# Scores three units ahead of the context products, and other work at two seams, in a layer of FFN, attention and FFN on one core

## The chip, the core and the metric

The kernel runs on one core of a Trainium2 chip. The metric is the device time of one execution in microseconds (us). The engines are TensorE (PE, whose weight loads are PEld), VectorE (DVE), ScalarE (ACT), GpSimd (POOL) and the queues that issue transfers, above all SyncE's (SP). Each takes its own instructions in the order written and waits on semaphores for the others.

## What is computed

x has 2 x 1024 tokens of 1024 numbers. The layer is: x += 0.5 * FFN(norm(x)); x += Attn(norm(x)); x += 0.5 * FFN(norm(x)).

- FFN: a product with a 1024 x 1024 weight and a bias, and low-rank products of 8 experts, of which the two with the largest gate logits count.
- Attn: q = h Wq (32 heads of 32), k = h Wk and v = h Wv (8 heads), rotary embedding on q and k, causal softmax of q k / sqrt(32), its product with v, then Wo. Four q heads share one k and v head, so there are 2 x 8 = 16 groups; below a group is called a head, as in the kernel's loop over n (NG = 16).

## The kernel before, in words

`build` (L1787) runs four stages, each in a block of its own: `ffn_stage` "f1", `qkv_stage`, `attention_stage`, `ffn_stage` "f2". At the end of a block all engines meet (in the profile a wait of one engine's sequencer at the line of `nc.Block()` or of the function's `with`), and only then does the next one begin. The two meetings that the change touches are called seams: f1 to qkv, and qkv to attention. Products are made of high and low parts: `split_products` (L73 to L77) issues three matmuls for one product.

**f1.** Tiles of 128 tokens. SP stores each result tile from `x_ring` to x1 in HBM (L331). At the end SP waits until all stores have landed (L337), so the meeting does too. In f1's last four tiles `early` gets the first four tiles of x1, normalized, for the next stage.

**qkv.** Chunks of 512 tokens: `step(b, ch, ...)` goes through b = 0, 1 and ch = 0, 1, and through o = 0 to 9 (8 blocks of Wq's columns, 2 of Wk's), then four tiles of v. PE first turns (transposes) the four `early` tiles (L959), each of which ACT and DVE split into high and low (L1040, L1178); then it does the first two products by pairs of tiles (`by_pairs`), and then, before o = 2, it turns tile 4 (`turn_h`, L951). For that DVE must have normalized tile 4 (L1172), which takes ACT's square root (`deviation`, L1035). ACT has 8 instructions ahead of that one in its order: `for j in range(KC)`, L1073 to L1075, which split the rows of Wk and Wv into their high parts as they land in the two buffers `wkv_raw`; POOL makes the low parts (L1122 to L1125), and SP loads rows j after the low part of j - 2 is done (L925). Wk is first needed at o = 8. At its end ACT loads the table of the exponential (L1113) and waits until v is stored (L1116).

**attention.** One head is 10 units, `units` (L1326): parts of the scores of four q heads (g = 0 to 3) with up to 512 queries and 128 or 256 keys. For a unit PE makes four scores (`scores`, L1587), ACT four exponentials (`exps`, L1678), POOL masks the units on the diagonal (0, 1, 2, 7, 8, 9; L1498), and PE makes the context products (`products`, L1604) and, after units 2 and 9, the row sums (`sums`, L1623 and L1627). The scores of a unit are made `AHEAD` units before its products:

```python
    PROBS = 6
    AHEAD = 2
        HELD = (1, 3, 5, 7)
```

Six units' exponentials have a place in `probs`. At step u, PE issues scores of unit u + AHEAD and, between them, rows of scores of the next heads (`slot_item`, L1576), whose maxima DVE takes (`row_maximum`, L69) from four PSUM banks, `SLOTS` = 4; the scores use `BANKS` = 3 others. Then it issues the products of unit u. Those of a unit in `HELD` wait for the next step and go with that unit's:

```python
                    if u - 1 in HELD:
                        products(n, u - 1)
                    if u not in HELD:
                        products(n, u)
```

POOL's order in a head is: mask of unit u + AHEAD at each step where there is one, `join` at u = 1 (L1526), `divide` at 2 and 8 (L1504), the additions of the exponentials of units 3 to 7 at u = 2, 3, 5, 6, 7 (`add`, L1519), `low_wo` at 9 (L1530). The sums after unit 9 need these additions. In the last head DVE makes them (L1765), and there are no more rows. The row maxima of a head come back, turned and negated, as two rows of its q (`load_rows`, L1442, two for each half of the queries). The scores of unit 0 wait for those of the first half, those of unit 3 for those of the second (L1584). The turn for the second half (`TURN_B`) is made at step 9 of the head before.

Of the kernel before, what the change touches and what calls it, by code (L numbers as in the profile page):

```python
# [99 lines left out]
def ffn_stage(nc, name, x_src, x_dst, base_b, consts, ident, chunk_loaded, prep=None, attn=None):  # L100
# [7 lines left out]
    with ExitStack() as ctx:  # L108
# [5 lines left out]

        fw = ffn_weights(nc, ctx, name)
# [13 lines left out]
        x_ring = sb("x_ring", [P, 4, D], F32)  # L129
# [148 lines left out]
        def _(sp):  # L278
# [33 lines left out]
            def step(i, t, u, more):  # L312
# [18 lines left out]
                sp.dma_start(x_dst[bass.ds(t * P, P), :], x_ring[:, u, :]).then_inc(stored[u], 16)  # L331
# [4 lines left out]
            for s in range(4):  # L336
                sp.wait_ge(stored[s], 16 * (NT // 4) + (16 if s == 3 else 0))  # L337
# [40 lines left out]
        def _(pe):  # L378
# [131 lines left out]
            run_tiles(pe, step)  # L510

# [267 lines left out]
def qkv_stage(nc, x_src, wq, early, heads, w, consts, ident, scr):  # L779
# [10 lines left out]
    with ExitStack() as ctx:  # L790
# [25 lines left out]
        v_out = sb("v_out", [P, 2, KV], F32)  # L816
# [43 lines left out]
        v_stored = [sem(f"v_stored{s}") for s in range(2)]  # L860
# [22 lines left out]
        def run_chunks(eng, step):  # L883

            with eng.Fori(0, B - 1, 1) as b:
                for ch in range(NCH):
                    step(b, ch, True)
            for ch in range(NCH):
                step(B - 1, ch, ch + 1 < NCH)

        @block.sync
        def _(sp):
# [23 lines left out]

            sp.dma_start(cos[:], consts["rope_cos"]).then_inc(const_loaded, 16)
            sp.dma_start(sin[:], consts["rope_sin"]).then_inc(const_loaded, 16)
            for j in range(KC):
                if j == WRAW:  # L920
                    sp.wait_ge(h_turned, TC + 1)
                    for slot in range(2):
                        load_x(TC + slot, slot)
                if j >= WRAW:
                    sp.wait_ge(wkv_lo_done, j - WRAW + 1)  # L925
                for cols, src in ((slice(0, KV), w["Wk"]), (slice(KV, 2 * KV), w["Wv"])):
                    sp.dma_start(wkv_raw[:, j % WRAW, cols], src[j * P:(j + 1) * P, :]).then_inc(wkv_loaded[j % WRAW], 16)
            with sp.Fori(TC // 2 + 1, NT // 2, 1) as i:
                for slot in range(2):
                    load_x(2 * i + slot, slot)  # L930
# [16 lines left out]
        def _(pe):  # L947
# [79 lines left out]
            for b in range(B):  # L1027
                for ch in range(NCH):
                    step(b, ch, b + 1 < B or ch + 1 < NCH, done=0 if b or ch else 2)

        @block.scalar
        def _(act):
# [40 lines left out]
            for j in range(KC):  # L1073
# [10 lines left out]
            def step(b, ch, more):  # L1084

                act.wait_ge(v_done, b * (NCH * TC) + (ch * TC + 1))
                for o in range(NO):
                    g = ch * NO + o
                    if not more and o and TURN_A in items_of(o):
# [9 lines left out]

                for s in range(TC):  # L1100
# [12 lines left out]
            act.activation(std[:], eps[:], ACT.Exp)  # L1113
            for s in range(2):
                act.wait_ge(out_stored[s], B * NCH * NO * 16 + 16)
                act.wait_ge(v_stored[s], B * NCH * TC * 8 + 16)  # L1116

        @block.gpsimd
        def _(pool):
            pool.memset(eps[:], EPS).then_inc(eps_set, 1)  # L1120
            pool.sem_inc(lo_done, 2)
            for j in range(KC):  # L1122
# [10 lines left out]
            def chunk_step(b, g):  # L1133
# [731 lines left out]
```

## Time and profile before

| what | us |
|---|---|
| runs shown: median of 3 (lowest to highest) | 1537.8 (1535.55 to 1539.06) |
| the profiled execution's own time | 1538.84 |
| its span in the trace | 1537.1 |
| PE busy in it | 1496.4 |
| POOL, DVE, ACT busy in it | 697.9, 952.0, 581.1 |

The span is from the first to the last instruction of the program. The rows of the trace give each instruction its start and its busy time in us; a matmul's end is modelled and lies behind the start of the next, so that where PE waits is read from the starts of its instructions, and a PE shown as busy may still wait a little between them. "xN" behind a row is the number of instructions merged in it. A bracket at a row's end is the engine's idle time before it and what released it. A table by windows shows stretches of the span with each engine's busy time and the clock that was granted to PE (1.00 is 2.4 GHz, 0.50 is 1.2 GHz).

### The profile page before, as it was taken

The numbers are of one execution on the slowest core, as the hardware profiler recorded it, in microseconds if no ns is written. First come the engines' busy times: TensorE is split into PE (matmuls) and PEld (weight loads), VectorE is DVE, ScalarE is ACT, GpSimd is POOL, SyncE is SP. The second block draws the span as 40 slices with busy tenths as digits, with TensorE's granted clock in tenths as the row PEclk, the third lists the DMA queues.
The fourth block names the chain that finished last, engine by engine and source line by source line (L and its number), as shares of the span: only waits on it lengthen the run. The fifth ranks groups of instructions, "written<-read, shape, count | busy, mean of one in ns | idle before, by whom it ended". The sixth has DMA issues, their size and how long they took to land. (4 is left out here: it accounts for less than half of the span.)

```text
span 1537.1 us, 25937 instructions
## 1 busy us (share of the span) xinstructions
PE 1496.4 (97%) x9184; PEld 1190.8 (77%) x9184; DVE 952.0 (62%) x2726; ACT 581.1 (38%) x1058; POOL 697.9 (45%) x384
## 2 busy tenths in 40 slices
PE   7899998899999989999999999999999999999999
PEld 7899998788888875555555555555489999999988
DVE  6545454564654767888888888888555434343433
ACT  4233332221211026666666666666632212121210
POOL 1232322442434337899989989999603001010100
PEclk9999999899999998999999999999999999999999
DMA  6323233433424352444333344430161212121201
GB/s 236 127 99 113 98 125 114 135 112 108 143 77 131 97 143 66 99 103 99 84 78 77 77 97 103 101 84 23 54 243 42 82 42 83 42 82 41 82 14 42
DMA packets 118725, 146.01 MB, mean 95 GB/s; under 512 B 40896, under 2 KB 77120, under 8 KB 118336
## 3 DMA queue, kind: packets, MB, share of 16 engines
q1 hardware_dynamic: 90304, 121.37, 27.6%
q10 hardware_dynamic: 28304, 23.14, 4.6%
q8 instruction: 66, 1.08, 0.3%
q14 instruction: 51, 0.42, 0.1%
HBM read 95.72 MB, written 53.51 MB: 97 GB/s over the span
## 5 line engine op out<-in xcount | busy, mean ns | idle before, releaser
L1678 ACT ACTIVATE at_probs<-ps 128x512 f32<-128x512 f32 (+1 forms) x640 | 315.0, 560 | 172.4 <-PE ps L1587 165.5
L69 DVE CUSTOM_DVE_ANT_0 ps<-ps,at_score_mask 128x512 f32<-128x512 f32 (+2 forms) x480 | 269.9, 621 | 25.9 <-PE ps L1576 22.2
L348 POOL TENSOR_TENSOR f_x_ring<-f_x_ring,f_half_bias 128x1024 f32<-128x1024 f32 x32 | 78.2, 2445 | 309.3 <-DVE f_h L634 303.1
L1519 POOL TENSOR_TENSOR at_added<-at_added,at_probs 128x2048 f32<-128x2048 f32 (+1 forms) x60 | 210.3, 3506 | 2.7 <-ACT at_probs L1678 0.7
L1604 PE MATMUL ps<-at_probs,at_vs 128*32 128x512 f32 (+3 forms) x1536 | 144.6, 494 | 0.3 <-POOL at_probs L1498 0.3
L75 PE MATMUL f_ps<-f_wt_hi,f_hT_hi 128*128 128x400 f32 (+1 forms) x384 | 134.1, 349 | 3.2 <-DVE f_hT_lo L638 3.2
L76 PE MATMUL f_ps<-f_wt_lo,f_hT_hi 128*128 128x400 f32 (+1 forms) x384 | 131.6, 343 | 0.0
L75 PE MATMUL ps<-f_wt_hi,f_hT_hi 128*128 128x400 f32 (+1 forms) x384 | 131.5, 343 | 0.0
L77 PE MATMUL f_ps<-f_wt_hi,f_hT_lo 128*128 128x400 f32 (+1 forms) x384 | 131.5, 342 | 0.0
L76 PE MATMUL ps<-f_wt_lo,f_hT_hi 128*128 128x400 f32 (+1 forms) x384 | 130.3, 339 | 0.0
L77 PE MATMUL ps<-f_wt_hi,f_hT_lo 128*128 128x400 f32 (+1 forms) x384 | 130.1, 339 | 0.0
L69 DVE CUSTOM_DVE_ANT_0 ps<-ps,at_score_mask,at_part_max 128x128 f32<-128x128 f32 (+3 forms) x240 | 120.9, 552 | 13.7 <-issue 13.5
L673 DVE TENSOR_TENSOR f_x_ring<-ps,f_x_ring 128x512 f32<-128x512 f32 x32 | 21.8, 690 | 137.7 <-PE ps L77 125.1
L1498 POOL TENSOR_SCALAR_AFFINE_SELECT at_probs<-at_probs 128x512 f32<-128x512 f32 (+1 forms) x96 | 80.8, 842 | 57.4 <-ACT at_probs L1678 57.4
L75 PE MATMUL ps<-wide_hi,shared 128*128 128x512 f32 x256 | 101.2, 395 | 1.6 <-DVEq L703 1.1
L1136 POOL TENSOR_TENSOR qkv_rot<-qkv_rot,qkv_sin 128x512 f32<-128x512 f32 x40 | 51.5, 1290 | 112.1 <-DVE qkv_rot L1222 112.1
L1587 PE MATMUL ps<-heads 98*128 98x512 f32 (+3 forms) x288 | 95.9, 377 | 5.4 <-PEq L1559 3.9
L77 PE MATMUL ps<-wide_hi,shared 128*128 128x512 f32 x256 | 99.9, 390 | 0.0
L76 PE MATMUL ps<-wide_lo,shared 128*128 128x512 f32 x256 | 99.8, 390 | 0.0
L352 POOL TENSOR_TENSOR wide_lo<-f_wq_raw,wide_hi 128x512 f32 (+1 forms) x16 | 23.6, 1474 | 161.4 <-ACT wide_hi L531 161.4
L1047 ACT ACTIVATE qkv_rope_hi<-qkv_rope 128x512 fp32r<-128x512 f32 x40 | 25.3, 632 | 185.2 <-DVE qkv_rope L1183 172.5
L1604 PEld LDWEIGHTS ps<-at_probs,at_vs 128*32 128x32 f32 x1536 | 40.3, 109 | 61.5 <-issue 44.7
(202 smaller groups left out, 3623.8 us busy)
## 6 DMA issues: line engine op xcount, KB each, us to landing
f_x_ring<-in_L_attn_resid SPq DMA_DIRECT2D x16, 512.0 KB, 3.6
x<-f_x_ring SPq DMA_DIRECT2D x16, 512.0 KB, 2.7
early<-x SPq DMA_DIRECT2D x16, 512.0 KB, 3.3
scr_q_hi<-qkv_rope_hi ACTq DMA_DIRECT2D x32, 256.0 KB, 2.0
scr_q_lo<-qkv_rope_lo ACTq DMA_DIRECT2D x32, 256.0 KB, 2.3
scr_ctx<-at_ctxn SPq DMA_DIRECT2D x32, 256.0 KB, 2.4
shared<-scr_ctx SPq DMA_DIRECT2D x16, 512.0 KB, 4.5
f_x_ring<-x SPq DMA_DIRECT2D x16, 512.0 KB, 3.7
```

The lines of the kernel that those rows point to most:

```text
L69: return dve.tensor_tensor_reduce(out=src[:, 0:keys], in0=src[:, 0:keys], in1=mask, scale=1.0, scalar=part_max[:, g, own] if c else -3.0e3 ...
L75: pe.matmul(out, stat_hi, mov_hi, start=start, stop=False)
L76: pe.matmul(out, stat_hi, mov_lo, start=False, stop=False)
L77: return pe.matmul(out, stat_lo, mov_hi, start=False, stop=stop)
L348: pool.tensor_tensor(x_ring[:, u, :], x_ring[:, u, :], half_bias[:], ALU.add).then_inc(bias_added, 1)
L1047: act.activation(rope_hi[:, g % 2, :], rope[:, g % 2, :], ACT.Copy).then_inc(hi_done, 1)
L1136: pool.tensor_tensor(rot[:, g % 2, :], rot[:, g % 2, :], sin[:, cols], ALU.mult).then_inc(sin_done, 1)
L1498: pool.affine_select(out=tile, in_=tile, compare_op=ALU.is_ge, fill=0.0, base=0, pattern=[[0, G], [0, count], [1, P]], channel_multiplier= ...
L1519: pool.tensor_tensor(added[:, heads, :], first, probs[:, (NU * n + u) % PROBS, heads, :], ALU.add).then_inc(added_done, 1)
L1587: last = pe.matmul(score_ps[x % BANKS][:, cols], ks[:, nm, j * P:(j + 1) * P], q_stack(n)[0:KROWS + 2, half, g, at], start=True, stop=True)
L1604: last = pe.matmul(ctx_ps[g * DH:(g + 1) * DH, at], vs[:, n % RING, j, :], probs[:, (NU * n + u) % PROBS, g, cols], start=j == 0, stop=u i ...
L1678: act.activation(probs[:, (NU * n + u) % PROBS, g, cols], score_ps[x % BANKS][:, cols], ACT.Exp, scale=SCALE).then_inc(exp_done, 1)
```

## The change

- attention: `AHEAD` is 3, `HELD` is (1, 3).
- f1 to qkv: the store of f1's last tile counts on a semaphore of its own, `x_stored`. f1 no longer waits for it; SP waits for it at the start of qkv, before its loads of constants, weights and x. PE makes 16 transposes of the identity at the end of f1. `x_ring` is placed first in f1's memory.
- in qkv: the high and low parts of Wk and Wv are made within the steps of the first chunk, j = 0 and 1 at o = 0, j = o + 1 at o = 1 to 6. SP loads tiles 6 and 7 of x ahead of rows 4 and 6 of the weights. Loops over b are written out.
- qkv to attention: SP waits for the stores of v at the start of attention, after two loads, and no more at the end of qkv; `v_out` is placed so that it outlives the stage. ACT loads the exponential's table before the last four tiles of v. PE makes 16 transposes at the end of qkv.

The diff, cut to its core:

```diff
@@ ffn_stage
+        x_ring = sb("x_ring", [P, 4, D], F32)
         fw = ffn_weights(nc, ctx, name)
...
-        x_ring = sb("x_ring", [P, 4, D], F32)
...
-                sp.dma_start(x_dst[bass.ds(t * P, P), :], x_ring[:, u, :]).then_inc(stored[u], 16)
+                own = x_stored if prep and isinstance(t, int) and t == NT - 1 else stored[u]
+                sp.dma_start(x_dst[bass.ds(t * P, P), :], x_ring[:, u, :]).then_inc(own, 16)
...
-                sp.wait_ge(stored[s], 16 * (NT // 4) + (16 if s == 3 else 0))
+                sp.wait_ge(stored[s], 16 * (NT // 4) + (16 if s == 3 and not prep else 0))
...
             run_tiles(pe, step)
+            if prep:
+                for _ in range(WARM):
+                    pe.transpose(hT_ps[:, 0, :], ident[:], ident[:])
@@ qkv_stage
-            with eng.Fori(0, B - 1, 1) as b:
+            for b in range(B):
                 for ch in range(NCH):
-                    step(b, ch, True)
-            for ch in range(NCH):
-                step(B - 1, ch, ch + 1 < NCH)
+                    step(b, ch, b + 1 < B or ch + 1 < NCH)
+        def weights_of(b, g):
+            if b or g >= KC - 1:
+                return ()
+            return (0, 1) if g == 0 else (g + 1,)
...
+            sp.wait_ge(x_stored, 16)
             sp.dma_start(cos[:], consts["rope_cos"]).then_inc(const_loaded, 16)
...
+                if j in (WRAW + 2, WRAW + 4):
+                    load_x(TC + j // 2, j // 2 % 2)
...
+            pe.wait_ge(cos_done, B * NCH * NO + 4)
+            for _ in range(16):
+                pe.transpose(ps[:, 2, 0:P], ident[:], ident[:])
...
-            for j in range(KC):
+            def high_weight(j):
                 act.wait_ge(wkv_loaded[j % WRAW], 32 * (j // WRAW + 1))
                 act.activation(wkv_hi[:, j, :], wkv_raw[:, j % WRAW, :], ACT.Copy).then_inc(wkv_hi_done, 1)
...
                     g = ch * NO + o
+                    for j in weights_of(b, g):
+                        high_weight(j)
...
+                if not more:
+                    act.activation(std[:], eps[:], ACT.Exp)
...
-            act.activation(std[:], eps[:], ACT.Exp)
             for s in range(2):
                 act.wait_ge(out_stored[s], B * NCH * NO * 16 + 16)
-                act.wait_ge(v_stored[s], B * NCH * TC * 8 + 16)
...
             def chunk_step(b, g):
+                    for j in weights_of(b, g):
+                        low_weight(j)
@@ attention_stage
-    AHEAD = 2
+    AHEAD = 3
...
-        HELD = (1, 3, 5, 7)
+        HELD = (1, 3)
...
                 load_v(r)
+            for stored in v_stored:
+                sp.wait_ge(stored, NT * 8 + 16)
```

## Rows read from the trace of the kernel before

**Rows 1.** The page's first part: busy time, share of the span, instructions.

```profile
PE 1496.4 (97%) x9184; PEld 1190.8 (77%) x9184; DVE 952.0 (62%) x2726; ACT 581.1 (38%) x1058; POOL 697.9 (45%) x384
```

**Rows 2.** Windows: stretch, length, busy PE, PEld, DVE, ACT, POOL, clock, DMA share, GB/s.

```profile
262.20:266.35 4.15, 0.00 (x0) 0.03 (x1) 0.57 (x2) 0.00 (x0) 0.10 (x1) 0.80 0.31 126
266.35:272.50 6.15, 6.15 (x33) 6.10 (x34) 2.45 (x2) 2.83 (x3) 0.00 (x0) 0.58 0.73 256
284.15:291.60 7.45, 0.00 (x0) 0.03 (x1) 1.78 (x4) 2.07 (x4) 4.54 (x4) 0.80 0.24 72
291.60:295.40 3.80, 3.80 (x13) 3.40 (x14) 3.70 (x6) 0.07 (x1) 2.52 (x2) 0.50 0.42 138
```

**Rows 3.** Timelines at the first seam; the row of 446.00 is eight transposes at full clock.

```profile
261.92 0.27 PE L77 MATMUL f_ps<-f_bt_hi,f_lowT_lo 128*128 128x224 f32 x1
...
262.80 0.35 SPq L331 DMA_DIRECT2D x<-f_x_ring  x1
...
269.45 1.22 DVE L1178 TENSOR_TENSOR heads<-qkv_ps,heads 128x1024 fp32r<-128x1024 f32 x1 [6.68 <-ACT heads L1040]
...
272.37 0.39 PE L75 MATMUL qkv_ps<-heads,wide_hi 128*128 128x256 f32 x1
...
446.00 1.04 PE L959 MATMUL qkv_ps<-ident,early 128*128 128x128 f32 x8
```

**Rows 4.** ACT and PE in qkv, up to the turning of tile 4.

```profile
268.39 1.02 ACT L1040 ACTIVATE heads<-qkv_ps 128x1024 fp32r<-128x1024 f32 x1 [8.91 <-PE qkv_ps L959]
...
289.47 0.28 ACT L1035 ACTIVATE qkv_std<-qkv_mv,qkv_eps 128x1 f32<-128x1 f32 x1
...
291.60 1.94 PE L959 MATMUL qkv_ps<-ident,early 128*128 128x128 f32 x8 [7.46 <-issue]
```

**Rows 5.** The second seam: windows, then ACT's and PE's timeline.

```profile
570.73:574.61 3.88, 0.00 (x0) 0.03 (x1) 0.00 (x0) 1.87 (x3) 0.59 (x2) 1.00 0.33 52
574.61:581.51 6.90, 6.76 (x23) 5.17 (x23) 1.80 (x11) 5.29 (x12) 1.35 (x2) 0.55 0.87 195
581.51:585.60 4.09, 4.09 (x15) 2.23 (x15) 1.76 (x8) 1.30 (x3) 3.06 (x2) 0.51 1.08 259
...
571.17 0.38 ACTq L1064 DMA_DIRECT2D scr_v<-qkv_v_out  x1
...
581.51 1.94 PE L1604 MATMUL ps<-at_probs,at_vs 128*32 128x512 f32 x8
```

**Rows 6.** One steady head as a window, from the end of one head's sums to the next.

```profile
886.12:919.69 33.57, 33.27 (x255) 19.23 (x251) 29.28 (x104) 21.61 (x45) 30.55 (x16) 1.00 0.40 88
```

**Rows 7.** PE and DVE in that head: products of two units, DVE's two longest pauses.

```profile
906.68 1.92 PE L1604 MATMUL ps<-at_probs,at_vs 128*32 128x512 f32 x16
...
909.38 0.63 DVE L69 CUSTOM_DVE_ANT_0 ps<-ps,at_score_mask,at_part_max 128x384 f32<-128x384 f32 x1 [0.87 <-issue]
...
919.92 0.72 DVE L1735 STREAM_TRANSPOSE at_sumT<-ps 128x512 f32<-128x512 f32 x1 [2.11 <-issue]
```

**Rows 8.** POOL's longest pause between two additions in that head.

```profile
904.94 0.68 POOL L1498 TENSOR_SCALAR_AFFINE_SELECT at_probs<-at_probs 128x512 f32<-128x512 f32 x1 [0.76 <-ACT at_probs L1678]
```

**Rows 9.** The rows that come back: issue, transfer time, and PE's next scores.

```profile
DMA to landing us min/median/max: 1.8/1.8/2.5
...
917.61 0.59 SPq L1442 DMA_DIRECT2D shared<-at_neg_lo  x1
...
919.69 0.44 PE L1587 MATMUL ps<-shared,heads 98*128 98x256 f32 x2
```

**Rows 10.** The last head on PE.

```profile
1101.88 0.96 PE L1587 MATMUL ps<-heads 98*128 98x512 f32 x3
...
1107.20 0.91 PE L1587 MATMUL ps<-heads 98*128 98x256 f32 x6
...
1108.68 1.71 PE L1604 MATMUL ps<-at_probs,at_vs 128*32 128x512 f32 x16
...
1111.39 1.04 PE L1623 MATMUL ps<-at_added,at_ones 128*32 128x512 f32 x8
```

More of the change, by code:

```diff
@@ L97, in flat, with ffn_stage @@
     return tile[:, :, :].rearrange("p c n -> p (c n)") if len(tile.shape) == 3 else tile[:, :]
-def ffn_stage(nc, name, x_src, x_dst, base_b, consts, ident, chunk_loaded, prep=None, attn=None):
+def ffn_stage(nc, name, x_src, x_dst, base_b, consts, ident, chunk_loaded, prep=None, attn=None, x_stored=None):
     RAW = 3
@@ L776, in _, with qkv_stage @@
             run_tiles(dve, step)
-def qkv_stage(nc, x_src, wq, early, heads, w, consts, ident, scr):
+def qkv_stage(nc, x_src, wq, early, heads, v_out, w, consts, ident, scr, x_stored, v_stored):
     NCH = T // HALF
@@ L815, in qkv_stage @@
         rope_lo = sb("rope_lo", [P, 2, HALF], F32R)
-        v_out = sb("v_out", [P, 2, KV], F32)
         q_stacks = [hT_hi[0], flat(wq_lo)[:, KC * HALF:].rearrange("p (b n) -> p b n", n=HALF)]
@@ L859, in qkv_stage @@
         v_copied = sem("v_copied")
-        v_stored = [sem(f"v_stored{s}") for s in range(2)]
         first_head_loaded = sem("first_head_loaded")
@@ L927, in _ @@
                     sp.dma_start(wkv_raw[:, j % WRAW, cols], src[j * P:(j + 1) * P, :]).then_inc(wkv_loaded[j % WRAW], 16)
-            with sp.Fori(TC // 2 + 1, NT // 2, 1) as i:
-                for slot in range(2):
-                    load_x(2 * i + slot, slot)
+            for t in range(TC + 4, NT):
+                load_x(t, t % 2)
             sp.wait_ge(v_done, (B * NCH - 1) * TC + 1)
@@ L1121, in _, with low_weight @@
             pool.sem_inc(lo_done, 2)
-            for j in range(KC):
+            def low_weight(j):
                 pool.wait_ge(wkv_hi_done, j + 1)
@@ L1140, in chunk_step @@
                         low_part(b, g)
-            with pool.Fori(0, B - 1, 1) as b:
+            for b in range(B - 1):
                 for g in range(NCH * NO):
@@ L1235, in _, with attention_stage @@
             run_chunks(dve, step)
-def attention_stage(nc, consts, ident, scr, wo, wo_src, heads, shared, ps):
+def attention_stage(nc, consts, ident, scr, wo, wo_src, heads, shared, ps, v_stored):
     RING = 3
@@ L1803, in build @@
     over = ExitStack()
+    x_stored = whole.enter_context(nc.semaphore("x_stored"))
+    v_stored = [whole.enter_context(nc.semaphore(f"v_stored{s}")) for s in range(2)]
     with ExitStack() as ctx:
         early = ctx.enter_context(nc.sbuf_tensor("early", [P, 4, D], F32))
-        ffn_stage(nc, "f1", x, x1, base_b, consts, ident, chunk_loaded, prep={"wq": wide, "early": early, "Wq": ins["L0_attn_Wq"], "copy": copy, **raw})
+        ffn_stage(nc, "f1", x, x1, base_b, consts, ident, chunk_loaded, prep={"wq": wide, "early": early, "Wq": ins["L0_attn_Wq"], "copy": copy, **raw},
+                  x_stored=x_stored)
         heads = over.enter_context(nc.sbuf_tensor("heads", [P, 2, KC, HALF], F32R, side="right"))
-        qkv_stage(nc, x1, wide, early, heads, attn_w, consts, ident, scr)
+        v_out = over.enter_context(nc.sbuf_tensor("v_out", [P, 2, NKV * DH], F32, side="right"))
+        qkv_stage(nc, x1, wide, early, heads, v_out, attn_w, consts, ident, scr, x_stored, v_stored)
     with ExitStack() as ctx:
@@ L1811, in build @@
         ps = ctx.enter_context(nc.psum_tensor("ps", [P, 8, HALF], F32))
-        attention_stage(nc, consts, ident, scr, wide, ins["wo_rows"], heads, shared, ps)
+        attention_stage(nc, consts, ident, scr, wide, ins["wo_rows"], heads, shared, ps, v_stored)
         over.close()
```

## Prediction, written before the changed kernel was run

> **What bounds the kernel now.** I read the page first: PE is busy for 97% of the span and no other engine for more than 62% [rows 1]. So time is won only where PE stands still, runs at the lower clock, or is spread out by waits between its instructions. I then read the windows around the seams and the timelines inside them, and last one head of attention.
>
> PE stands still in three places. Between f1 and qkv it has nothing for 4.15 us, and then works for 6.15 us at a mean clock of 0.58 [rows 2]. Its last matmul starts at 261.92; the last store of x is issued at 262.80 [rows 3]. Inside qkv it stands for 7.45 us and then runs 3.80 us at clock 0.50 [rows 2]. Between qkv and attention it stands for 3.88 us and then works until 585.60 at 0.55 and 0.51 [rows 5].
>
> In attention one head takes 33.57 us. PE shows 33.27 us busy, POOL 30.55, DVE 29.28, ACT 21.61 [rows 6]. PE's figure hides waits, as its ends are modelled. DVE's rows are what it waits for: within the head DVE pauses for only 33.57 - 29.28 = 4.29 us. The two largest pauses are 2.11 us before the sums of unit 9, and 0.87 us right after PE has gone through the products of two units, 16 instructions in 1.92 us, in which no row is made and DVE uses up its four banks [rows 7].
>
> **First seam, 3.2 us.** The meeting now waits for the landing of the last store, issued at 262.80. After the change the last to arrive is PE itself: its 16 transposes cost, by the eight in 1.04 us at full clock, about 0.11 us each when pipelined, so 1.8 us, to about 263.9 [rows 3]. The store's issue ends at 263.15 and lies beside it. A meeting takes 0.6 to 0.9 us; nearest to it is the gap from the store's landing to 266.35. I take 0.75: PE begins qkv at 264.6, not at 266.35, 1.75 us earlier. Then the first pair of products waits for two tiles to be split: eight transposes (1.04), one copy by ACT (1.02) [rows 4], two subtractions by DVE (1.22 each) [rows 3], 4.5 us in all with the hops: 269.15, where it was 272.37 [rows 3]. That is 3.2 us. If the clock still falls, only the 1.75 us remain. SP waits for the landing before it loads constants; that is no later than it was, so it costs nothing. The 16 transposes have the store's landing as their cover before the change and none after it: they are the price of the clock, 1.8 us, already in the sum. Did the meeting wait for anything else that I don't see, the lower end is 0.
>
> **The pause inside qkv, 9.35 us.** ACT comes to the square root for tile 4 only at 289.47, after its eight parts of Wk and Wv; tile 4 is turned at 291.60 [rows 4]. Moved into the steps, six of the eight stand behind that root. Tile 4 of x can be normalized long before 284. So all 7.45 us go, and with them the 3.80 us at half clock, which cost half of it, 1.90 [rows 2]. What is late next: Wk at o = 8, six blocks of Wq's columns later. Every copy is made a step ahead of POOL's subtraction and SP's next load, and ACT, POOL and SP have pauses in each step; SP is now held by the waits for tiles 6 and 7, with only weights behind them. Cover gone, one weight late would cost about a step. I take 9.35, bounds 7.45 and 9.35. The written-out loops I cost at nothing: branches stand beside PE's work.
>
> **Second seam, 2.5 us.** ACT issues the last store of v at 571.17 [rows 5], and the meeting waits for its landing. Now PE's 16 transposes, to 572.5, come last, and attention begins at about 573.5, not 574.61, 1.1 us earlier. With three units ahead there are 16 exponentials, not 12, before the first products. ACT spends 5.29 us on 12, 0.44 each [rows 5]; PE is let go three banks before the end, after 13: 0.5 + 13 x 0.44 = 6.2 us, so products at 579.7, where they were at 581.51: 1.8 us. The head then ran at half clock until 585.60, 4.09 us [rows 5], of which 2 us come back if the clock holds. If it falls, the rows between the scores take some 0.5 more as well. That is 1.3 to 3.8; since PE is only half busy in that prologue I take 2.5, midway.
>
> **The steady heads, 13.05 us.** Units 5 and 7 no longer wait for the next one, so PE gives 8 product instructions at a time where it gave 16, about 1 us in place of 1.92. Four waiting rows of about 0.63 us cover that, and the pause of 0.87 us goes [rows 7]. DVE sets the pace in this stretch, so I take it whole; the 2.11 us before the sums stay, as the order around unit 9 is unchanged. The added cost is two more changes between kinds of work on PE, 0.1 to 0.2 us each, hidden by DVE; without that cover 0.35 us a head. POOL gets its masks' inputs a unit earlier and loses its pause of 0.76 us [rows 8], so its 30.55 us don't bind at 32.7. Fifteen heads have rows beside them: 15 x 0.87 = 13.05 us. The bounds for a head are a loss of 0.35 and a gain of 1.5 (DVE's pauses other than the 2.11 cut to some 0.7).
>
> **The last head, 1.9 us.** No rows there: ACT paces the scores. From 1101.88 to 1111.39 are 9.51 us [rows 10]. After: four scores (1.3), products of 5 (0.95), four scores (1.5), products of 6 (0.95), then those of 7 to 9, 1108.68 to 1111.39, 2.71: 7.4. Four wider scores at its step 0 give 0.2 back. Between 0 and 2.5.
>
> **Sum.** 3.2 + 9.35 + 2.5 + 13.05 + 1.9 = 30.0 us. The profiled execution took 1538.84, 1.0 above the median of the runs: 1508.8. f2 is PE at full clock and moves along with it.
>
> **A rule against the change.** In the stretch 266.35 to 272.50 PE had nothing but transposes until 272.37, and its mean clock was 0.58, so it rose from 0.50 to 1.00 before the stretch ended [rows 2, 3]. The Trainium skill, "TensorE: Matmul & The Clock Gate", Part 4, says that the full clock doesn't engage for transposes, which don't count as PE busy. By the trace they do count; by the rule the 16 would be time spent for nothing, and the seams would stay cold, as in the second rival.
>
> **The rivals.**
> - *Nothing in the steady heads.* The pause of 0.87 us goes and comes back elsewhere, before the sums, since PE, DVE and POOL all lie within 10% of each other [rows 6]. Then 1538.84 - 16.95 = 1521.9.
> - *The clock falls at both seams all the same.* For it: PE is half busy in attention's prologue. Against it: pauses of under 1 us, where those of 3.88 us and more had it fall. The first seam gives 1.75, the second 1.3: 1538.84 - 27.35 = 1511.5.
> - *More in the heads.* DVE never pauses but for 2.11 + 0.6 us: 32.0 us a head, 1.5 saved each: 1538.84 - 16.95 - 22.5 = 1499.4.
> - *Slower: the rows that come back.* The scores of unit 3 are now made at step 0, right behind the sums. They wait for two small transfers: issued at 917.61, 1.8 us on the way, so 919.4, against PE's first scores at 919.69 [rows 9]. The margin is 0.3 us. If DVE comes to that turn four rows (2.6 us) later against PE, every head waits 2.3 us: 1538.84 - 16.95 + 15 x (2.3 - 0.87) = 1543.3. From 2.0 us a head on it decides. Against it: the turn itself waits for DVE, so PE can't run far ahead.
> - *The change doesn't do what it says.* A meeting may wait for another landing, and a mask made sooner may hold POOL's additions; gains and losses then cancel.
>
> **How the numbers follow.** Chances: forecast 0.55; nothing in the heads 0.17; clock falls 0.13; more in the heads 0.10; slower 0.03; cancelling 0.02. The range reaches from 1499 to 1523, over the first three and most of the fourth. What a measurement tells from no change is about 0.2%, 3 us. Faster by more: 0.95; within: 0.02; slower: 0.03.
>
> **What would show it.** PE's last f1 matmul and first qkv transpose under 3 us apart, at clock 1.00; no pause of 7 us before tile 4; the first products of attention 14.4 us earlier than at 581.51 (3.2 + 9.35 + 1.8), near 567; heads of 32.7 us with DVE's pause of 0.87 gone and that of 2.11 kept; POOL without the 0.76. Wrong it would be if heads stay at 33.6, if PE pauses before unit 3's scores (L1587) behind the sums, or if unit 9's sums wait for POOL.

## The result, and the profile after

The changed kernel takes 1519.2 us by the median of 4 runs (1518.3 to 1520.0), the kernel before on the same chip 1536.7: a ratio of 0.9887, 95% interval 0.9872 to 0.9902. The gain is 17.5 us, where 30.0 were forecast (1508.8); the range of 1499 to 1523 holds it. The profiled execution took 1518.7 us, its span is 1517.0. The gain between the two profiled executions is 20.1, and 3.0 of that lie in f1, ahead of everything that the prediction counted: PE waits once for DVE before the small transpose of `low_s`, for 3.14 us in the trace before and for 1.64 in the one after, and behind the longer wait the clock is at 0.5 for 3.4 us. f1's instructions up to there are the same, only the place of `x_ring` in memory isn't. Of the twelve traces with the changed kernel's f1 two have that fall (e5 and e6), of the two with the f1 of before both (e2 is the other). So the change may have a part in it; two traces are too few to tell. The 3.0 us are kept apart below.

By the page's first part PE is busy for 1487.0 us, where it was 1496.4 [rows 1]. It has 32 instructions more (the transposes) and yet is busy 9.4 us less: matmuls at the lower clock count as busy for longer, and there are fewer of them.

The windows of the changed kernel that answer to [rows 2] and [rows 5], and one head, which answers to [rows 6] (columns as there; the break leaves out qkv, the last line is the head):

```profile
259.16:261.51 2.35, 1.75 (x18) 1.54 (x15) 0.58 (x2) 0.00 (x0) 0.10 (x1) 1.00 0.38 157
261.51:266.14 4.63, 3.69 (x32) 3.44 (x32) 2.41 (x3) 3.46 (x4) 0.00 (x0) 1.00 0.63 222
...
557.84:558.73 0.89, 0.00 (x0) 0.03 (x1) 0.00 (x0) 0.00 (x0) 0.59 (x2) 1.00 0.58 87
558.73:567.46 8.73, 8.45 (x28) 6.20 (x28) 1.81 (x11) 7.34 (x16) 2.45 (x3) 0.63 0.95 199
867.89:900.98 33.09, 32.77 (x255) 19.53 (x251) 29.37 (x104) 21.26 (x45) 30.55 (x16) 1.00 0.41 89
```

The first seam is warm now. The second is not: attention begins after only 0.89 us, and still its prologue has a mean clock of 0.63. A head is 0.48 us shorter, not 0.87. PE's timeline at the end of f1 and inside qkv:

```profile
259.00 1.91 PE L514 MATMUL f_ps<-ident 128*128 128x128 f32 x16
...
266.14 0.39 PE L75 MATMUL qkv_ps<-heads,wide_hi 128*128 128x256 f32 x1 [0.95 <-DVE heads L1196]
...
277.76 0.49 PE L967 MATMUL qkv_ps<-ident,early 128*128 128x128 f32 x3
...
491.24 0.33 PE L1001 MATMUL qkv_ps<-heads 96*128 96x128 f32 x1 [0.82 <-DMA qkv_wkv_raw<-in_score_mask]
```

How it is read, with the 3.03 us of f1 taken off each time (f1's last product starts 3.03 us earlier, 258.89 against 261.92):

- qkv begins at 261.51, 1.81 us sooner; its first pair of products at 266.14, where it was 272.37: 3.20 sooner.
- Tile 4 is turned at 277.76, without a pause, where it was 291.60: another 7.6. The stretch behind it, which ran at half clock before, gives 1.8 more (the same matmul stands at 295.46 before and at 279.81 after). Together 9.4.
- The row at 491.24 is a wait that the kernel before hardly had: PE stands before the first row of the next stage's first head. The transfers that bring that head are issued as much earlier as PE is (the mask at 481.22, where it was 496.82), but the one that lands last, the mask, takes 9.97 us where it took 9.01. It costs 1.0 us of what had been won: the distance to the kernel before falls from 15.65 us ahead of it to 14.64 behind it.
- Attention begins 15.9 us earlier than at 574.61 as the clock shows it, 12.8 without f1's part: 3.2 + 9.4 - 1.0 + 1.2.
- The first products of attention come 8.73 us after its start. Before it was 6.90, and I had forecast 6.2.

DVE in the steady head, answering to [rows 7]:

```profile
887.67 0.70 DVE L69 CUSTOM_DVE_ANT_0 ps<-ps,at_score_mask 128x512 f32<-128x512 f32 x1 [0.29 <-PE ps L1596]
...
901.22 0.72 DVE L1755 STREAM_TRANSPOSE at_sumT<-ps 128x512 f32<-128x512 f32 x1 [2.02 <-issue]
```

The pause of 0.87 us is down to 0.29 and not gone, that before the sums (2.11 us before) is still there, and POOL's pause before a mask [rows 8] is gone: POOL's longest is now 1.70 us before the join of unit 1, waiting for PE's products. In this head DVE's pauses fell from 4.29 us to 3.72 and its busy time rose by 0.09; the head lost 0.48. What can't be seen in these rows is what sets a head's length now, and which of the two edits of attention did it. The runs answer the second and part of the first.

In what follows a head's length is taken from the end of one head's last sums to the end of the next head's (the last one runs to the first product behind attention). By this measure the 14 steady heads took 470.7 us before and 464.7 after (33.62 and 33.20 each), the first one 42.04 and 43.59, the last one 26.88 and 27.10.

### The profile page after: what moved, and what is told of

It reads as the page before. It is cut to its first block and busy times, and to the rows that moved or that the text cites. A ratio compares the mean times of both kernels' runs of the same rounds, so it can differ in the third digit from the quotient of the medians.

```text
span 1517.0 us, 25951 instructions
## 1 busy us (share of the span) xinstructions
PE 1487.0 (98%) x9216; PEld 1192.2 (79%) x9216; DVE 954.8 (63%) x2726; ACT 576.2 (38%) x1058; POOL 700.9 (46%) x384
## 5 line engine op out<-in xcount | busy, mean ns | idle before, releaser
L1698 ACT ACTIVATE at_probs<-ps 128x512 f32<-128x512 f32 (+1 forms) x640 | 311.1, 560 | 169.4 <-PE ps L1607 164.1
L1624 PE MATMUL ps<-at_probs,at_vs 128*32 128x512 f32 (+3 forms) x1536 | 152.1, 500 | 0.7 <-POOL at_probs L1518 0.7
L1607 PEld LDWEIGHTS ps<-heads 98*128 98x128 f32 x288 | 52.9, 197 | 44.4 <-ACT at_probs L1698 25.1
```

Source lines behind the costliest of these rows:

```text
L1607: last = pe.matmul(score_ps[x % BANKS][:, cols], ks[:, nm, j * P:(j + 1) * P], q_stack(n)[0:KROWS + 2, half, g, at], start=True, stop=True)
L1624: last = pe.matmul(ctx_ps[g * DH:(g + 1) * DH, at], vs[:, n % RING, j, :], probs[:, (NU * n + u) % PROBS, g, cols], start=j == 0, stop=u i ...
L1698: act.activation(probs[:, (NU * n + u) % PROBS, g, cols], score_ps[x % BANKS][:, cols], ACT.Exp, scale=SCALE).then_inc(exp_done, 1)
```

## The experiments

### Which part gave what: e1 and e2

e1 is the changed kernel with attention as it was; e2 is the kernel before with attention's edits alone.

```diff
 e1, on the changed kernel            e2, on the kernel before
-    AHEAD = 3                        -    AHEAD = 2
+    AHEAD = 2                        +    AHEAD = 3
-        HELD = (1, 3)                -        HELD = (1, 3, 5, 7)
+        HELD = (1, 3, 5, 7)          +        HELD = (1, 3)
```

> The changed kernel with attention as before (two units ahead, four held). My theory: the parts add up. Read from the two traces, attention begins 3.2 + 9.4 - 1.0 + 1.2 = 12.8 us earlier through the seams' edits (the 1.0 is the new wait in qkv's last chunk), and with two units ahead its first head costs what it did before, so the gain over the kernel before is 12.5 to 13.5 us: about 1523.7 us. Rival A: the loss in the first head (1.55 us) comes from the seam, not from the third unit ahead; then the gain is 11.3. Rival B: the seams' edits give less by themselves, because attention's own edits shift the first store of v or the meeting: under 10. Heads of 33.6 us in every case.

> The kernel before with attention's two edits alone (three units ahead, two held). My theory: 14 heads that each give 0.42 us, a last head and a first head that lose what they lose in the changed kernel: a gain of 4 to 6 us, about 1532 us, heads of 33.15 us. As forecast blind it would have been 13.05 + 1.9 + 1.8 = 16.8 us. Rival: the heads are faster by 0.87 us when they start at another phase of the transfers, a gain over 10 us. Rival: the first head loses nothing here since the cold start of the old seam is paid anyway; then the gain is 6 to 7.

e1: 1526.9 us against 1537.8, ratio 0.9926 (0.9904 to 0.9949), a gain of 10.9. e2: 1530.9 us, ratio 0.9944 (0.9924 to 0.9963), a gain of 6.9. Together 17.8, against the change's 17.5: the parts add up, within their intervals. e1's gain is under what I expected, and its trace shows where: its first head takes 41.73 us, as before, so rival A is wrong, but its last takes 30.24 us instead of 26.88, with the clock at 0.5 twice, from 1076.7 and from 1090.3, each time for 3.4 us. e2 gained a little more than the 4 to 6 us that I expected: its steady heads take 463.7 us for 14, 0.50 less each, the first head 1.1 us more than before and the last 1.0 us less. So the seams give some 11 to 13 us, attention's edits the other 5 to 7.

### Which edit of attention: e3 and e4

Both are the changed kernel with one of the two taken back.

```diff
 e3                                   e4
-        HELD = (1, 3)                -    AHEAD = 3
+        HELD = (1, 3, 5, 7)          +    AHEAD = 2
```

> The changed kernel with units 5 and 7 held again (1, 3, 5, 7), scores still three units ahead. Theory of the prediction: the pause of 0.87 us of DVE comes from the held pair, so it comes back and heads are at 33.5 to 33.6 us: 5 to 7 us slower than the changed kernel. Rival: the third unit ahead alone gives the gain, since PE's scores stand ready and ACT's late exponentials no longer stop it; then it is within 2 us of the changed kernel, and so is the pair's pause in heads of 33.1 us.

> The changed kernel with scores two units ahead, units 5 and 7 still not held. Theory of the prediction: the pair's products are split in two, DVE's pause of 0.87 us goes, but products of units 5 and 7 come a step earlier behind their own exponentials, which lie only two units back, so PE waits for ACT or for POOL's masks in steps 5 and 7; that wait is worth what the pause was: heads between 33.1 and 33.6 us. In the first head it gains 1.5 us against the changed kernel (12 exponentials before the first products, not 16). Rival: the third unit isn't needed at all, heads of 33.1 or under, and the kernel is 1 to 3 us faster than the changed one.

e3: 1525.7 us, ratio 0.9926 (0.9903 to 0.9950). e4: 1518.1 us, ratio 0.9875 (0.9844 to 0.9905). A head's window in e3 and in e4, and under it the row of DVE that answers to the one with 0.87 in [rows 7], first for e3:

```profile
839.32:873.01 33.69, 33.40 (x251) 19.70 (x250) 29.32 (x104) 21.55 (x45) 30.44 (x16) 1.00 0.38 87
...
862.59 0.63 DVE L69 CUSTOM_DVE_ANT_0 ps<-ps,at_score_mask,at_part_max 128x384 f32<-128x384 f32 x1 [0.87 <-issue]
```

and then for e4:

```profile
864.91:897.98 33.07, 32.79 (x254) 19.37 (x250) 29.42 (x104) 21.41 (x45) 30.64 (x16) 1.00 0.38 89
...
884.72 0.70 DVE L69 CUSTOM_DVE_ANT_0 ps<-ps,at_score_mask 128x512 f32<-128x512 f32 x1 [0.33 <-PE ps L1596]
```

With four units held, the pause of 0.87 us is back to the hundredth, and the third unit ahead gives the steady heads nothing: 33.81 us each over 14, against 33.65 in e1. With two held and scores only two units ahead it is down to 0.33, and the heads take 33.15 us, as in the changed kernel. **The whole gain in the heads is that of the two holds given up.** The third unit costs in the first head: it took 43.5 us with it (e3, and 43.59 in the changed kernel) and 41.1 to 41.7 without it (e4, e1), about 2 us. In the last head it gives back 1.2 where the clock holds (25.5 in e3, 26.7 in e4). For e4 the rival was right about the heads, and my expectation that units 5 and 7 would then wait for ACT was wrong. That e4 as a whole is the faster kernel isn't shown: its four runs lie at 1514.3, 1514.9, 1521.3 and 1522.4 us, and its interval covers the changed kernel's.

### Who paces a steady head: e5 to e8

Each is the changed kernel with one engine's work in 12 or 14 heads made longer or shorter. e6 leaves out the spreading of the reciprocals in heads 2 to 13, so their context isn't divided by their own sums.

```diff
 e5, DVE, behind the rows of step 6; e8 the same on POOL
+                    if 0 < n < NG - 1 and u == 6:
+                        dve.memset(spare[:], 0.0)
 e6, DVE, in reciprocal
-                dve.transpose(recip[:], recipT[:].broadcast_to([P, HALF // DH, DH])).then_inc(recip_done, 1)
+                if 1 < n < NG - 2:
+                    dve.sem_inc(recip_done, 1)
+                else:
+                    dve.transpose(recip[:], recipT[:].broadcast_to([P, HALF // DH, DH])).then_inc(recip_done, 1)
 e7, PE, in products, ahead of those of unit 0
+                if u == 0 and 0 < n < NG - 1:
+                    for g in range(G):
+                        pe.matmul(ctx_ps[g * DH:(g + 1) * DH, :], vs[:, n % RING, 0, :], probs[:, NU * n % PROBS, g, :],
+                                  start=True, stop=True)
```

> The changed kernel with one more operation of DVE in 14 heads, a memset of a spare tile of 128x512 behind the rows of step 6; nothing waits for it. In the changed kernel a head takes 33.06 to 33.1 us in its shortest form, with DVE 29.37 and PE 32.77 us busy. Theory A (DVE still paces the rows, as the prediction had it): the head grows by the whole of that operation, 0.3 to 0.6 us as its row will show. Theory B (with the pair's pause gone PE is the bound, its products, scores and rows running at the pace of their own columns): the operation is hidden in DVE's remaining 3.7 us of pauses and the head grows by under 0.1 us.

> The changed kernel in which heads 2 to 13 leave out the transpose that spreads the reciprocals of the sums (two in each head, 0.7 us each), so that the context of these heads isn't divided by its own sums; POOL's multiplication and all waits stay. Theory A (DVE paces the head): up to 1.4 us less a head, 31.7. Theory B (PE is the bound): under 0.2 us less, and DVE's pauses grow by the 1.4.

> The changed kernel in which PE makes the four products of unit 0 twice in 14 heads (the same result, 0.43 us more at full clock if four instructions take what the four of a 512-wide group do in the trace). Theory A (DVE paces): hidden but for what lies behind DVE's own waits: the head grows by under 0.15 us. Theory B (PE is the bound): it grows by 0.35 to 0.45 us.

> The changed kernel with one more operation of POOL in 14 heads, a memset of a spare tile of 128x512 at step 6 (0.53 us by the like row of the prologue). POOL is busy for 30.55 of 33.09 us and stands 1.7 us before the join, where it waits for PE. Both theories: hidden, under 0.1 us a head. Rival C (POOL's additions set when the sums come, so that POOL shares the pace): 0.3 to 0.5 us a head.

One run each; the times (1522.3, 1517.8, 1534.8 and 1520.5 us) aren't compared, since f1's fall stands in two of them (e5 and e6), so only the heads are read. A window of one of the shorter heads in each, in the order e5, e6, e7 and e8:

```profile
838.34:871.64 33.30, 32.83 (x254) 19.46 (x251) 29.59 (x105) 21.24 (x45) 30.53 (x16) 1.00 0.38 89
```

```profile
868.96:901.93 32.97, 32.65 (x255) 19.47 (x251) 28.18 (x102) 21.25 (x45) 30.61 (x17) 1.00 0.39 90
```

```profile
880.65:914.55 33.90, 33.57 (x263) 19.75 (x259) 29.39 (x104) 21.22 (x45) 30.59 (x16) 1.00 0.38 87
```

```profile
835.14:868.42 33.28, 32.90 (x255) 19.66 (x251) 29.37 (x104) 21.21 (x45) 31.02 (x17) 1.00 0.39 89
```

Against 33.09: e5 makes a head 0.21 us longer, e6 0.12 shorter, e8 0.19 longer, e7 0.81 longer here. On the mean of all 14 steady heads (33.20 in the changed kernel) e5 and e8 cost 0.14 each, e6 gives 0.11, e7 costs 1.25 (about 0.8 in the first and in the last six, 1.2 to 2.2 in the seven between). Read with the busy time of DVE: in e5 it grew by 0.22 us, less than the memset's 0.485, whose ends overlap the rows beside it, and the head by about as much. In e6 it fell by 1.19 and the head by a tenth of that; DVE's pauses grew from 3.7 to 4.8 us. So of more work on DVE most of what adds to its busy time is paid, and less of it gives almost nothing: something else holds a head at 33.0 us. Of POOL's 0.52 us 0.19 is paid, against my expectation.

That PE's own work is the floor isn't shown. PE's busy figure counts modelled ends. From start to start a 512-wide score or row takes 0.23 us in that head and four 512-wide products side by side 0.45; by such steps all of PE's instructions come to some 29 us of the 33.09 (an estimate from the trace's starts). The rest are 0.1 to 0.2 us at each change between kinds of work, and waits: the weight loads of the scores wait for ACT's exponentials for 3.1 us in that window. No run changed ACT's work, so ACT's exponentials, which free the scores' three banks, stay an untested rival for the pace.

Where the rest of e7's loss comes from is seen in part on DVE. The first row is from the changed kernel, at the row behind the products of unit 0; the second is its like in e7:

```profile
871.67 0.57 DVE L69 CUSTOM_DVE_ANT_0 ps<-ps,at_score_mask 128x384 f32<-128x384 f32 x1 [0.52 <-PE ps L1596]
```

```profile
885.26 0.57 DVE L69 CUSTOM_DVE_ANT_0 ps<-ps,at_score_mask 128x384 f32<-128x384 f32 x1 [1.36 <-PE ps L1596]
```

While PE gives products, DVE uses up its four banks and then stands, and what it then lacks, PE waits for later. My reading is that a longer group of products is paid once on PE and again in part when DVE has to catch up, and that the holds work in the same way: 16 products in 1.92 us left DVE without rows for 0.87 us, twice 8 in 1.0 us leave it for 0.29. Neither theory holds as a whole: DVE's added work costs less than theory A says and more than theory B, DVE's removed work gives what theory B says, and PE's added work costs twice what theory B says.

The seven heads of e7 that lose 1.2 us and more have another wait. Each of them begins with one of 0.5 to 1.2 us at its first score, for the negated rows that come back:

```profile
707.25 0.50 PE L1607 MATMUL ps<-shared,heads 98*128 98x512 f32 x1 [0.74 <-DMA shared<-at_neg_lo]
```

This is the wait of the prediction's slower rival. In the changed kernel PE stands there in one head alone, for 0.40 us.

### No hold at all: e11

```diff
-        HELD = (1, 3)
+        HELD = ()
```

> The changed kernel in which no unit's products are held back to the next step (units 1 and 3 too). By the four kernels already run, giving up two of the four holds is worth 0.49 us a head, and the third unit ahead is worth nothing; the reason that I draw from the traces is that PE then gives its products in shorter groups and DVE isn't left without rows. If so, the pauses of DVE of 0.5 us (behind the products of units 0 and 1) shrink too: heads of 32.8 to 33.0 us. Rival: unit 1 is held because its mask and the join of POOL lie there; PE then waits for POOL and a head is 0.5 us or more longer. Since PE's own work is near its floor (32.97 us a head with 1.4 us of DVE's work taken away), nothing under 32.7 is expected.

One run: 1536.7 us, as slow as the kernel before. A head:

```profile
844.70:879.22 34.52, 33.46 (x251) 19.30 (x251) 29.42 (x104) 21.48 (x45) 30.47 (x16) 1.00 0.36 85
```

The rival's time is right, and more than right: 1.4 us more a head. Its reason is so in part: the weight loads of PE's products wait twice for POOL's masks in that window, 0.7 us in all, and not at all in the changed kernel's. POOL stands before the join for 2.9 us (1.7 in the changed kernel), but there it is POOL that waits for PE, and PE's scores stand behind ACT's exponentials for 4.6 us (3.1). The loss is 0.3 us up to the first half's sums, 0.3 in steps 3 and 4, 0.8 in step 5, and none behind it. In step 5 PE waits for DVE, in nearly every head and not in the changed kernel:

```profile
863.61 0.50 PE L1596 MATMUL ps<-heads 96*128 96x512 f32 x1 [0.71 <-DVE at_row_max L69]
```

Behind the products of unit 3, now given by themselves, DVE had stood for 1.25 us (at 859.06). So there a group given early leaves DVE without rows, and "shorter groups are better" holds for units 5 and 7 alone. Whether the hold of unit 1 or that of unit 3 matters more was not run.

### The transposes at the seams: e9

e9 is the changed kernel without the 16 transposes behind f1 and the 16 behind qkv.

```diff
-            if prep:
-                for _ in range(WARM):
-                    pe.transpose(hT_ps[:, 0, :], ident[:], ident[:])
...
-            for _ in range(16):
-                pe.transpose(ps[:, 2, 0:P], ident[:], ident[:])
```

> The changed kernel without the 16 transposes behind f1 and the 16 behind qkv. In the changed kernel's profile the first 16 run from 259.00 to 260.91, qkv begins at 261.51 and its first products at 266.14, and the clock stays at 1.00 until attention's prologue. Theory A (the transposes hold the clock): qkv begins 0.5 to 0.9 us earlier, since now the issue of the last store of x (about 260.1) comes last, but the clock falls behind f1 and the first products come 1.5 to 3 us later than with them. Theory B (the short pause is enough, the transposes are 1.8 us spent for nothing, which is also what comes out if transposes don't count as work for the clock): no fall at the first seam, first products 0.5 to 0.9 us earlier. At the second seam the clock falls in the prologue with them as without: attention begins about 1 us earlier by both.

One run, 1514.7 us. Behind f1:

```profile
259.92:261.84 1.92, 0.00 (x1) 0.03 (x1) 0.59 (x2) 0.00 (x0) 0.10 (x1) 1.00 0.25 100
261.84:266.48 4.64, 3.69 (x33) 3.46 (x33) 2.42 (x3) 3.47 (x4) 0.00 (x0) 1.00 0.66 234
```

PE stands for 1.92 us and the clock doesn't fall. From f1's last product's end to the first pair it is 6.56 us, where the changed kernel takes 6.98 (259.16 to 266.14): theory B, 0.4 us gained by leaving them out. The same edit in e12 below did have a fall of 3.4 us there, and took 7.03. So the first set is worth next to nothing: 6.98 us with it, against 6.56 without it when the clock holds and 7.03 when it falls. At the second seam the clock falls without them 0.4 us into attention, with them 2.3 us into it; the first products come 8.73 us after the start in both, and attention begins 0.6 us sooner after qkv's last product (1.98 us, not 2.6).

### Holding the clock in attention's prologue: e10

e10 has two units ahead (as e4), two transposes behind each of the prologue's eight scores, and the mask's load moved ahead of the first head's queries.

```diff
-    AHEAD = 3
+    AHEAD = 2
...
                     scores(0, u, g)
+                    for _ in range(2):
+                        pe.transpose(slot_ps[0][:, 0:P], ident[:], ident[:])
...
+            sp.dma_start(score_mask[:, HALF:MASK], consts["score_mask"]).then_inc(first_head_loaded, 16)
             load_queries(0, first_head_loaded)
             load_keys(0, first_head_loaded)
-            sp.dma_start(score_mask[:, HALF:MASK], consts["score_mask"]).then_inc(first_head_loaded, 16)
```

> The changed kernel with scores two units ahead, with two transposes of PE behind each of the first eight scores of attention's prologue (into a slot that the rows use later), and with the load of the mask ahead of the first head's queries instead of behind its keys. Theory A (the clock falls in the prologue since PE is only half busy between ACT's exponentials): a score and two transposes are 0.43 us against ACT's 0.48, so the clock holds, the first head takes 2.5 to 3.5 us less than the 41.14 us of the like kernel without them, and the wait before the first row in qkv's last chunk goes from 0.8 to 0: 1514.5 us or less by the median, 3.5 to 4.5 us under the kernel with two units ahead alone (1518.07). Theory B (the fall comes from the pause before attention, 0.9 us, and not from the half-busy prologue, or transposes don't count): the clock falls at the same place, the transposes then cost up to 0.2 us each, and the first head is 1 to 2 us longer.

1512.8 us by the median, ratio 0.9844 (0.9827 to 0.9860). That is 5.3 us under e4's median, but e4's runs lie 8 us apart; what the transposes do is read from the traces. The prologue in e4, and behind it in e10 a window nearly as long (both from attention's start; in e10 it takes in the first products too):

```profile
558.46:565.36 6.90, 6.67 (x23) 4.97 (x23) 1.81 (x11) 5.30 (x12) 1.35 (x2) 0.64 0.92 198
```

```profile
559.94:566.44 6.50, 6.50 (x47) 5.16 (x47) 2.22 (x14) 5.29 (x12) 1.66 (x3) 1.00 0.93 189
559.94:598.93 38.99, 38.14 (x280) 23.32 (x280) 29.70 (x113) 25.58 (x53) 30.36 (x16) 1.00 0.33 71
```

Theory A is right: the granted clock stays at 1.00 from 15.8 us to the end of the span, and the first head takes 38.99 us where it took 41.14, a little less of a gain than the 2.5 to 3.5 us expected. In attention nothing was added but small transposes between the scores, and e12 below, with the mask's load in its old place, holds the clock there too, so here they do keep it up. The rule of the Trainium skill that the prediction weighed ("TensorE: Matmul & The Clock Gate", Part 4) says they would not; by it the prologue of e10 should have been as cold as e4's, and the measurement decides. The mask's move did nothing: the wait before the first row is 1.0 us, since now the keys land last, at 492.40, 10.0 us after their issue; in the changed kernel the mask had come 10.0 us after its own. That time isn't fixed: the last of the seven took 8.9 us in e9 and 7.9 in e12, and there PE has no such wait. What sets it stays open.

### The best of it: e12

e12 is e10 with the mask's load back in its place, without the transposes behind f1, and with the rows of qkv's last chunk begun one product later.

```diff
-            if prep:
-                for _ in range(WARM):
-                    pe.transpose(hT_ps[:, 0, :], ident[:], ident[:])
...
-                            if 1 <= c <= len(own):
-                                row_item(own[c - 1])
+                            late = 2 if o == ROW_FROM else 1
+                            if late <= c < len(own) + late:
+                                row_item(own[c - late])
```

> The changed kernel with two units ahead and with two transposes behind each of the first eight scores of attention's prologue, as in the run that held the clock through the whole of the second seam (1512.78 by the median); the mask's load is back in its place, the 16 transposes behind f1 are gone (those behind qkv stay), and the rows in qkv's last chunk start one product later in their first block. Theory: from the look without transposes, qkv begins 0.4 us sooner behind f1 and the clock holds; the wait of 0.8 to 1.0 us before the first row is covered by the 0.75 us of one product: together 1.0 to 1.3 us, so 1511.5 to 1512 us by the median and at least 24 us under the kernel before. Rival A: the clock falls behind f1 in part of the executions, since nothing keeps PE at work there; then 1513 to 1515 us, and a wider spread. Rival B: the wait before the first row moves with the rows, since DVE is behind; then the gain is 0.4 us.

1511.5 us by the median of 5, ratio 0.9842 (0.9825 to 0.9859) against the kernel before. That beats both kernels: the changed one had 0.9887 (0.9872 to 0.9902), and the intervals don't meet. From e10 it can't be told apart. In its profile the wait before the first row is gone, but the later rows aren't shown to be the reason: the mask landed at 489.29, and the first row, at 490.75, would have come at about 490.06 without the product put ahead of it. And the clock fell behind f1, after PE had stood from 258.94 to 260.86:

```profile
260.86:265.97 5.11, 5.11 (x32) 5.11 (x33) 2.45 (x2) 2.94 (x3) 0.00 (x0) 0.67 0.71 252
```

The same pause of 1.92 us as in e9, and another outcome; the fall costs 0.5 us here (5.11 against 4.64), since the stretch behind it mostly waits for DVE and ACT. Rival A is right in its mechanism; its price was small. Two of e12's five runs took 3 us more than the others (1514.5 and 1514.7 against 1511.1 to 1511.5); they have no trace. A fall in f1, worth 3.0 us, would fit them, and so this isn't rival A's range coming true.

## Why the prediction was right, and where it failed

The range held the result; the likeliest value was 10.4 us too low. Luck had a part in the range. The forecast started from an execution that had f1's fall, and the changed kernel's profiled one did not: with it, it would stand near 1522, at the range's upper end. In the same way the sign "first products near 567" was met (567.46) with 3.0 us of f1's in it; without them the products came 11.0 us earlier, not 14.4. The terms against what the traces show, f1's 3.0 us left out:

| term | forecast | measured |
| --- | --- | --- |
| first seam, to the first pair | 3.2 | 3.2 |
| pause inside qkv | 9.35 | 9.4 |
| wait for the first head's loads | none | -1.0 |
| second seam: attention begins | 1.1 | 1.2 |
| second seam: to the end of the first head | 1.4 | -1.55 |
| steady heads | 13.05 | 5.9 |
| last head | 1.9 | -0.2 |
| sum | 30.0 | 17.0 |

(The measured terms and f1's 3.0 give 20.0, the two profiles 20.1. The forecast of 13.05 was for 15 heads, the first one among them; the measured 5.9 are 14 heads, and the first head stands in the row above.)

- **First seam: right, by its own steps.** The start came 1.81 us sooner (1.75), the pair 3.20 (3.2). Only the reason given for the transposes was wrong. I wrote that they "are the price of the clock"; e9 shows a seam without them that stays warm, e12 one that doesn't, and either way the first pair comes within half a microsecond of the same place.
- **The pause inside qkv: right.** Wk and Wv, moved behind the root, were never late. What I missed is the wait at qkv's end. I had costed the loops' moves and the weights, and not the loads for the next stage. They moved along with PE, but the last of them took 9.97 us, not 9.01, and had no margin: before, it landed at 505.84 and the first row began at 505.92.
- **Second seam: the step "16 exponentials, not 12: 0.5 + 13 x 0.44 = 6.2 us" failed.** It left out the clock, and it let PE go too early. The prologue took 8.73 us at a mean clock of 0.63. I had set a rival for a falling clock but priced it at 1.3 us of gain, because I took [rows 5], which were cold as well, as if three units ahead would add only ACT's time to them. e10 shows what the warm clock is worth there (2.15 us in the first head), e3 against e1 what the third unit costs (1.7). My evidence against a fall, "pauses of under 1 us", looked at whole pauses and not at PE's share of work. The clock isn't all of it: in four traces (before, changed, e4 and e10) the first products begin within 0.25 us of the start of the last exponential, and not after the last but three. In e10, warm and with 12 exponentials, that is 5.60 us after attention's start, where my step gives 0.5 + 9 x 0.44 = 4.5. With four more of 0.44 us it would be some 7.4 (an estimate, with e10's transposes in it): of the 2.5 us missed, about half is the release and half the clock.
- **Steady heads: the step "DVE sets the pace in this stretch, so I take it whole" failed.** The pause did come from the pair of held units, as forecast, and did go (0.87 to 0.29, and back to 0.87 in e3). But a head gained 0.42 on average. 0.29 of the missing 0.45 is the part of the pause that stayed: four waiting rows didn't cover eight products. The rest is that DVE isn't the only bound. The runs show one at about 33.0: with two of DVE's transposes removed, 1.2 us of its busy time, a head still takes 32.97. A forecast of 32.7 lay below it, and so did the rival of 32.0. Whose bound it is isn't shown, PE's own or that of PE and ACT together; that PE's 33.27 us hide waits was right. The rival "nothing in the steady heads" was right that the engines lie close together, wrong that the pause comes back before the sums (2.11 before, 2.02 after), and its time of 1521.9 is nearer to the result than mine.
- **The last head: the terms on PE were right, the clock wasn't in them.** Where the clock holds it takes 25.5 us (e3, e9 and others with three units ahead), 1.4 less than before. In the profiled execution it fell at 1073.1, while ACT paced the scores, and all of the gain was gone. This fall comes in some executions and not in others.
- **The slower rival** had its wait: the weight load of unit 3's first score stands for the negated rows in nearly every head, 0.2 us in most and 0.7 once. The margin of 0.3 us was nearly right. The wait doesn't grow here, but it did in e7, to 1.2 us, so the chance of 0.03 wasn't a chance of nothing.

## What to carry to other kernels

When two or three engines are each within 10% of a stage's length, removing the longest pause of one can be worth much less than the pause; test the distance to the next bound by taking work away from the first engine before you count on it, and do it for each engine that could be that bound. An edit that works by its groups (how many products PE gives in a row) and one that works by its lead (how many units ahead) should be timed apart: here one gave all of the gain in the steady heads, and the other cost 2 us in the first head and gave back 1.2 in the last. Where PE has to run at another engine's pace for several microseconds, fill the gaps between its instructions with small transposes into a free bank and look whether the granted clock holds, rather than put them all ahead of the pause.

## What the runs showed of the hardware

- The clock fell with no pause of PE over 1 us near it: in the changed kernel 2.3 us into the prologue, after a pause of 0.89 us, while PE made a 512-wide score of 0.2 us for each exponential of 0.48 us. With two transposes of 0.11 us more per score it stayed at 1.00 (e10 and e12).
- The same pause of 1.92 us, with the same instructions on both sides, left the clock at 1.00 in e9 and was followed by 3.4 us at 0.5 in e12, from 1.3 us behind its end. One execution doesn't settle what a seam does to the clock.
- Falls lasted 3.4, 6.8 or 10.2 us in all these traces. In the prologue it was 10.2 in the kernel before, the changed one, e2, e5 and e9, and 6.8 in e1, e3, e4, e6, e7, e8 and e11.
- 0.43 us more of products in front of a group cost a head 0.8 us and more, while DVE's pause behind them grew from 0.52 to 1.36 us.
- The last of the seven transfers that bring attention's first head landed 7.9 to 10.0 us after its issue in the traces (e12, e10 and the changed kernel), for the same seven of 64 to 512 KB.
